# Routing and experts moved into the last image's attention, in one block

## The reference

```
x  = x + deform_conv(group_norm(x))        # 3x3 taps, each with its own (dy, dx), bilinear
t  = x as 1024 tokens
t  = t + attention(layer_norm(t))          # one causal head of 64, 1024 x 1024 scores
n  = layer_norm(t)
logits = n @ gate_w.T + gate_b             # 1024 tokens x 32 experts
probs  = softmax(logits, over the tokens)
topv, topi = top_k(probs, 8)               # each expert chooses 8 tokens
pooled[e] = sum_k topv[k, e] * n[topi[k, e]]
out[e] = gelu([pooled, 1] @ w1[e]) with 1 appended, @ w2[e]     # 65 -> 256 -> 64
t[topi[k, e]] += topv[k, e] * out[e]
```

## Time and profile before

| | us |
|---|---|
| median of 3 runs | 507.71 (504.94 to 508.09) |
| profiled execution, device time | 507.9 |
| its span in the profile | 506.1 |
| busy: PE, DVE, ACT, POOL | 416.1, 345.3, 289.8, 159.5 |
| last `back` (end of the last convolution) starts | 389.98 |
| logits of the last image start on ACT | 445.71 |
| first instruction of `route` | 452.15 |
| first matmul of `mlp` | 473.64 |
| first matmul of `combine` | 492.63 |
| last add | 499.81 |

### The profile page before, as it was taken

How to read it: one execution, slowest core, us unless ns; L and a number is a source line. 1 busy time by engine, 2 the same in 40 slices (tenths; PEclk the granted TensorE clock), 3 DMA queues, 4 the chain that set the end, 5 groups by cost and what they waited for, 6 DMA issues and landing times. The chain is left out here.

```text
span 506.1 us, 14009 instructions
## 1 busy us (share of the span) xinstructions
PE 416.1 (82%) x5845; PEld 307.5 (61%) x5845; DVE 345.3 (68%) x478; ACT 289.8 (57%) x531; POOL 159.5 (32%) x119
## 2 busy tenths in 40 slices
PE   1606985899999999999999999999999788227574
PEld 0204572576777677767767776767867556226274
DVE  3234668777898889889889989888896653213034
ACT  2323264778787687778677776877676456022100
POOL 2006007106534535472354446040640430310000
PEclk9756597999999999999999999999999969755589
DMA  9598969788787778588867789868730000039208
GB/s 221 97 208 189 222 144 231 179 205 177 188 205 177 177 183 186 123 207 195 186 160 174 175 176 207 198 158 198 181 71 12 2 2 12 1 70 229 84 3 166
DMA packets 33698, 75.61 MB, mean 149 GB/s; under 512 B 22365, under 2 KB 25373, under 8 KB 27293
## 3 DMA queue, kind: packets, MB, share of 16 engines
q1 hardware_dynamic: 28750, 72.68, 62.7%
q10 hardware_dynamic: 4880, 1.98, 1.7%
HBM read 64.74 MB, written 7.01 MB: 142 GB/s over the span
## 5 line engine op out<-in xcount | busy, mean ns | idle before, releaser
L1073 DVE TENSOR_TENSOR wring<-stage 96x640 f32<-96x640 f32 x192 | 173.0, 943 | 32.5 <-ACT stage L869 28.5
L1248 PE MATMUL psum<-wring,zring 96*64 96x160 f32 (+4 forms) x1728 | 124.8, 293 | 6.4 <-DVE wring L1073 6.4
L1248 PEld LDWEIGHTS psum<-wring,zring 96*64 96x64 f32 x1728 | 104.6, 141 | 20.9 <-issue 15.9
L1035 DVE TENSOR_REDUCE negmax<-psum 128x1 f32<-128x128 f32 (+3 forms) x64 | 48.3, 754 | 34.5 <-PE psum L1097 34.4
L1215 PE MATMUL psum<-kern,img 64*32 64x192 f32 x1536 | 58.5, 343 | 9.0 <-ACT zring L876 8.4
L876 ACT ACTIVATE zring<-psum 96x768 f32<-96x768 f32 x64 | 51.4, 803 | 23.0 <-PE psum L1215 21.4
L902 ACT ACTIVATE pT<-psum 128x512 f32<-128x512 f32 (+2 forms) x96 | 46.0, 483 | 28.4 <-PE psum L1105 28.1
L961 ACT ACTIVATE prob<-psum,negmax 128x128 f32<-128x128 f32 (+3 forms) x64 | 47.0, 734 | 22.9 <-DVE negmax L1035 18.4
L1093 PE MATMUL psum<-kT,qT 64*128 64x128 f32 (+4 forms) x400 | 51.7, 361 | 4.6 <-DVE kT L1030 1.5
L1105 PE MATMUL psum<-const,prob 128*128 128x128 f32 x288 | 50.5, 287 | 3.2 <-ACT pT L902 3.0
L866 ACT ACTIVATE stage<-stage,const 96x384 f32<-96x384 f32 x64 | 38.9, 608 | 20.5 <-DMA stage<-near 20.3
(11 more groups left out here) (120 smaller groups left out, 525.9 us busy)
## 6 DMA issues: line engine op xcount, KB each, us to landing
stage<-near SPq DMA_DIRECT2D x192, 288.0 KB, 5.5
w<-in_w SPq DMA_DIRECT2D x1, 2080.0 KB
tok<-in_x SPq DMA_DIRECT2D x8, 256.0 KB, 5.2
images<-img SPq DMA_DIRECT2D x8, 256.0 KB, 3.8
w<-in_w SPq DMA_DIRECT2D x1, 2048.0 KB
img<-img SPq DMA_DIRECT2D x7, 256.0 KB, 3.0
near<-tents SPq DMA_DIRECT2D x32, 45.0 KB
shifts<-offT SPq DMA_DIRECT2D x8, 128.0 KB, 6.4
```

Of the source, the lines that this page charges most:

```text
L1035: dve.tensor_reduce(negmax[:, t:t + 1], score_rows(t, a), AX.XY, ALU.max, negate=True).then_inc(s["mx"], 1)
L1073: dve.tensor_tensor(rows[:, ky, :, place], stage[0:KX, q % STG, ky, 1:, :], stage[0:KX, q % STG, ky, 0, :].unsqueeze(1).to_broadcast([KX, ...
L1248: ins = pe.matmul(psum[C * e:C * e + C, 2 + half, (lo % 16) * W:(lo % 16 + n) * W], zring[0:KX, q % ZRING, i % 2 * 2 + e, ky * C:(ky + 1) ...
```

## The change

There is one block. `route`, `mlp` and `combine` become the classes `Pooled` and `Experts`, whose steps are put into the last image's tables or behind the branch.

- Images are grouped 0 to 3, 4 and 5, 6 and 7 (`GROUPS`). Groups 0 and 1 (called `many`) go through choice, gather, layer 1, Gelu and the transposes inside the last image's table; their layer 2, the move, the combination and the stores come behind the branch.
- Group 2 (images 6 and 7, called `single`) does everything behind the branch. The last image's logits go from PSUM straight into rows 32 to 63 of `logits[2]`, without a DMA; the router of the last image is two matmuls of 512 columns instead of eight of 128.
- The weights are loaded by SP as soon as the last image's convolution is over, into the memory of `stage` and `wring` that it leaves. POOL zeroes `zring` and a part of `stage` there. The biases of layer 1 come as a table `b1` of 1 MB and are added by DVE; in exchange layer 1 has 64 rows and uses both halves of the array. A gather writes 16 columns (half the experts) to each half of PSUM.
- The order of the steps of all images is new in all five tables. Steady images keep the same order on POOL; on PE, ACT and DVE some neighbours change places. For image 0, ACT has `rows` 0 behind the two `tent` steps, and `rows` 1, `rows` 2 and `raw` of image 1 behind `columns` 0, which were ahead of it. For the last image, ACT has `query` ahead of image 6's `out`, and so has PE `score` 0.

```diff
@@ keep_logits @@
             sync.wait_ge(s["lg_sb"], ONE + a + 1)
+            if alone(a):
+                sync.sem_inc(s["lg_ok"], 64)
+                return
@@ act_attention @@
+                if alone(a):
+                    act.activation(by_token(logits[2][E:2 * E, :]), by_half(psum[0:E, 4:6, :]), ACT.Identity,
+                                   bias=kbias[0:E, 3:4]).then_inc(s["lg_sb"], 1)
+                    return
@@ the sync stream @@
+                    if at in table(SP_AT, b)["weights"]:
+                        sync.wait_ge(f["mm"], 2 * NG4)
+                        sync.wait_ge(f["w_ok"], K * NG4)
+                        load_weights(sync)
...
                 unless_near(sync, sync_again)
+                sync_store(sync)
+                store_last(sync, 0)
@@ new in run_all @@
+        def pe_end(pe):
+            many.layer2(pe, 0)
+            many.move(pe, 1)
+            for n in range(3):
+                pe_weigh(pe, n)
+            pooled[2].turn(pe, 0, 0)
+            pe_weigh(pe, 3)
+            pooled[2].gather(pe, 1)
+            for n in range(4, 6):
+                pe_weigh(pe, n)
+            pe.wait_ge(pooled[2].s_pT, 1)
+            single.layer1(pe)
+            for n in range(6, len(strips)):
+                pe_weigh(pe, n)
+            pe.wait_ge(s_x, len(strips))
+            for n in range(4):
+                single.turn(pe, n)
+            single.layer2(pe, 0)
+            single.move(pe, 1)
...
+            for h in range(2):
+                for t in range(NT // 2 * h, NT // 2 * h + NT // 2):
+                    ins = pe.matmul(psum[:, 2 + h, t % 4 * EXP[2]:(t % 4 + 1) * EXP[2]], pm[2][0:E * (last - first), t * P:(t + 1) * P],
+                                    eo[2][0:E * (last - first), :], start=True, stop=True)
+                ins.then_inc(s_y2, 1)
+        def act_end(act):
+            act.activation(spare[:, 1:2], ident[:, 0:1], ACT.Exp)
+            choices[2].exponentials(act)
+            act.wait_ge(s_zero, 2)
+            many.keep(act, 1, copy)
+            act.activation(spare[:, 2:3], ident[:, 0:1], ACT.Gelu)
+            pooled[2].keep_turned(act, 0, 0)
+            pooled[2].keep(act, 1)
+            for n in range(4):
+                single.gelu(act, n)
+            for n in (2, 3):
+                single.keep_turned(act, n, copy)
+            store_last(act, 1)
+        def dve_end(dve):
+            dve_choose(dve, 2, 0)
+            dve.wait_ge(s["pt"], ONE + B * NCK)
+            many.keep_out(dve, 0)
+            for step in range(1, 5):
+                dve_choose(dve, 2, step)
+            for n in range(len(strips)):
+                dve_add(dve, n)
+            for n in range(4):
+                single.add_bias(dve, n)
+            for n in range(2):
+                single.keep_turned(dve, n, dve.tensor_copy)
+            single.keep_out(dve, 0)
+            single.keep(dve, 1, dve.tensor_copy)
...
```

More of the change, by code:

```diff
@@ L75 @@
-    dict(
[L76 to L89, removed]
@@ L90 @@
-    dict(
[L91 to L104, removed]
+        turn=[-16447],
@@ L105 @@
 ACT_AT = (
     dict(
[L107 to L119, removed]
@@ L148 @@
-    dict(
[L149 to L161, removed]
+        raw=[-12735],
@@ new lines @@
+        leave=[-5039],
+        tent=[-3791, -3551],
+        columns=[-2431, -191, 753, 1185, 1234, 1505, 1729, 1811],
+        rows=[-3535, -1007, -687, 929, 1233, 1521, 1809, 1812],
+        half=[1810, 2001],
+        norm=[2465],
+        query=[2577],
+        exp=[2625, 2705, 2769, 2802, 3025, 3169, 3457, 3553],
+        prob=[2657, 2801, 2977, 3105, 3170, 3409, 3458, 3473, 3537, 3569, 3681, 3745],
+        out=[3793],
+        norm2=[4145],
+        logits=[4177],
+        choose=[],
+        pooled=[],
@@ new lines @@
+        many=[]),
+    dict(
+        raw=[-400],
+        leave=[176],
+        tent=[416, 512],
+        columns=[880, 960, 1248, 1344, 1488, 1616, 1680, 1776],
+        rows=[944, 1152, 1232, 1456, 1600, 1664, 1744, 1792],
+        half=[1936, 2288],
+        norm=[2640],
+        query=[2688],
+        exp=[2768, 2816, 2928, 3152, 3216, 3440, 3520, 3648],
+        prob=[2880, 3104, 3136, 3360, 3424, 3456, 3504, 3552, 3616, 3664, 3712, 3744],
+        out=[3792],
+        norm2=[4128],
+        logits=[4208],
+        choose=[],
+        pooled=[],
+        many=[]),
@@ new lines @@
+    dict(
+        raw=[-431],
+        leave=[209],
+        tent=[417, 497],
+        columns=[881, 930, 1234, 1361, 1425, 1553, 1650, 1729],
+        rows=[929, 1153, 1233, 1601, 1649, 1713, 1809, 2001],
+        half=[1905, 2353],
+        norm=[2673],
+        query=[2801],
+        exp=[2804, 2851, 2947, 3169, 3505, 3793, 3922, 3969],
+        prob=[2852, 2946, 3394, 3745, 3746, 3889, 3921, 3923, 3953, 4241, 4242, 4577],
+        out=[4626],
+        norm2=[6241],
+        logits=[7329],
+        choose=[],
+        pooled=[],
+        many=[]),
@@ L285, in constants @@
+    dict(
+        second=[1],
+        tents=[1106],
+        load=[1121, 1122, 1137, 1233, 2241, 2242, 2243, 2257],
+        logits=[10081],
+        weights=[4497]))
 def constants():
```

980 lines of the change are left out of this document (579 added, 401 removed).

## The result

The changed kernel takes 504.22 us in the median of 20 runs (501.16 to 508.83), the kernel before 511.21 us beside it. The ratio is 0.9905 (95% interval 0.9877 to 0.9933); a second set of six runs gave 0.9897 (0.9851 to 0.9943). So it is faster, by 1%, where 2.3% was forecast (496 us against a profiled execution of 507.9). The profiled execution took 502.84 us, span 501.0. The kernel before itself measured 3.5 us more here than the 507.7 that the forecast started from.

What follows compares the result with a forecast made beforehand. PE was taken to bound the middle, with a serial 59.9 us after image 7's logits as target. Logits at 446.2 + 1.1 + 1.4 = 448.7, plus tail 45.6, gave span 494.3; with 1.8 around it 496 us, range 488 to 504.

Steps and rivals of the forecast that it cites:

- The middle: Steady stretch bound by PE: same instructions in nearly the same order, so 0 us, bounds -3 and +4.
- The start: Images 0 and 1: image 1's statistics come later behind reordered ACT copies; net loss 1.1 us, bounds -1 and +3.
- The attention: Last image's attention: earlier `query` saves 2.4 us, inserted steps add 2.8; sum +0.4, bounds -2 and +6.
- The norm chain: Last image's norm up to its logits: inserted steps and wider logits push the end; +1.4 with the attention, bounds 0 and +9.
- The tail: Everything behind image 7's logits: branch, experts, combination and stores take 45.6 us, bounds 39 and 50.
- The Exp table: ACT behind the branch: a 1.28 us table load on the path; with the skill's 1.38 us drain, 497.4 us.
- 3 (a full branch): Branch ahead of the tail: waited out in full on ACT and PE, 5 us instead of 3; 498 us, chance 0.08.
- 1 (PE at full clock): Branch and tail: PE stays at 1.00, saving 2.0 us in layer 2 and 3.6 in the move; 490 us, chance 0.13.
- 2 (the inserted steps delay the attention by 6 us): Last image's attention: inserted steps delay it at half clock, +6 us; 502 us, chance 0.11.
- 4 (PE waits for DVE's products, 517): Middle: the new order makes PE wait up to 0.7 us at 32 pieces, 21 us; 517 us, chance 0.07.
- 5: Whole kernel: the change does little, half of rivals 4 and 2 together; 505 us, chance 0.08.
- The signs: Wrong if PE idles over 10 us between 100 and 380, `out.7` passes 440, or an engine stands over 5 us behind the branch.

Runs made afterwards that it cites:

- a0: The changed kernel run again unchanged; ratio 0.9897 to the kernel before, median 502.2 us.
- t1: The changed kernel with the tail's code inside the taken branch on every engine, and a second copy in the other arm; ratio 0.9668, 492.0 us.
- t4: The kernel of t1 with one added wait holding TensorE idle for 3.84 us ahead of layer 2; ratio 0.9864, 501.0 us.
- m1: The changed kernel with the gathering and expert steps of images 0 to 5 moved behind the last image's attention; ratio 1.0388, 526.6 us.
- h10: The changed kernel with the kernel before's order up to the end of the last convolution; ratio 0.9773, 497.6 us.
- h10b: The kernel of h10 run again; ratio 0.9777, 495.5 us.
- c1b: The kernel of c1 run again; ratio 0.9595, 487.8 us.
- c3: The changed kernel with the old order everywhere, last image included, and the tail inside the taken branch; ratio 0.9666, 490.7 us.
- x01: The kernel before with only the changed kernel's order tables, none of its new steps; ratio 1.0076, 513.2 us.
- t3: The changed kernel with the tail inside the taken branch on ScalarE alone; ratio 0.9966, 506.5 us.
- t1b: The kernel of t1 run again; ratio 0.9753, 496.2 us.
- t2: The changed kernel with the tail inside the taken branch on TensorE alone; ratio 0.9682, 492.3 us.
- s1: The changed kernel with image 0's first two column copies on ScalarE put back behind image 1's raw copy; ratio 0.9812, 499.2 us.
- c2: The kernel of t1 with the one start-order entry of s1 undone; ratio 0.9663, 491.3 us.
- c1: The changed kernel with h10's old order in front and t1's tail inside the taken branch; ratio 0.9657, 492.1 us.

## Why the prediction was wrong

The step that failed is the middle, put at 0. It covered image 7's convolution too, and there the new order costs 3.2 us in the changed kernel's trace. The whole miss in the trace, span 501.0 where the sum had 494.3, is made up of: start +0.6 (1.7 for a forecast 1.1), steady images -0.4, image 7's convolution +3.2, attention and norm chain +1.4 (2.8 for 1.4), tail +2.0 (47.6 for 45.6).

- **The middle (0).** I let PE's waits stay as they were, since the order hardly changes. One new wait of PE for DVE's products, 1.56 us, and in four of the nine traces the half clock behind it, make the last convolution 1.8 to 3.2 us longer than in before. Over seven traces of the new tables (changed, a0, t1 to t4, m1) the last back is at 393.6 to 396.0, with the old front (before, h10, h10b, c1b, c3) at 388.2 to 390.0; 391 was forecast.
- **The start (+1.1, bounds -1 and +3).** Right in direction and within its bounds against the trace of before: DVE's L514 moves from 38.62 to 42.26 (forecast 41.5), and the first back from 76.6 to 78.3. But with the same order in front the other traces have it at 73.4 to 75.0, so the start may cost 3 to 5 us; the wait of `mix` for ACT's copies is 16.1 us against 9.7 in h10 and 8.2 in before.
- **Start and middle in time.** Together they are +6.4 us (h10 and h10b against the changed kernel), or +3.9 by x01, for a forecast +1.1. With the old front the kernel measures 497.6 and 495.5, beside the forecast's 496. That is in part luck: h10's attention and norm chain are 2.6 us longer than before's where I had 1.4, and its last back is at 390.0 where I had 391.
- **The attention (+0.4, bounds -2 and +6).** The size is within its bounds: 43.4 to 44.6 us in the changed kernel, a0, t1 to t3 and both h10, and 46.2 in t4, with 42.9 before, so +0.5 to +3.3 (in the changed kernel +1.7). The reason is not borne out: I priced the inserted steps, and m1 is no faster without those on PE and ACT.
- **The norm chain (+1.4 with the attention).** From the last back to the logits it is 59.0 us in the changed kernel and in a0, 57.7 in t1, 60.0 in t4 and 56.2 before: the two steps together are +1.5 to +3.8, in the changed kernel +2.8. The first layer 1 started at 442.97, not before 438, and took 3.67 us at half clock where I had 1.8.
- **The tail (45.6, bounds 39 and 50).** The sum was right, its parts less so, and they cancelled: 47.6 and 44.2 in two traces of the changed kernel, 45.6 and 45.7 in h10 and h10b. Inside it, the branch was put at 3.0 on either engine: in the traces that jump it is 2.3 to 3.1 on ACT, and on PE 3.3 to 4.1 plus 1.6 to 2.0 inside layer 2. Layer 2 at 4.0 was right (1.50 and 2.51). The move ended 14.7 us behind the logits (forecast 13.5), and three weighs took 5.49 us at half clock where I had 2.7 at full, so they ended at 21.7 (forecast 18.0); what follows took 25.9 us where I had 27.6.
- **The Exp table.** The load takes 1.28 us in the rows. By the Trainium skill, "ScalarE: Activation LUTs", section "What ACT_TABLE_LOAD costs", 1.38 us of drain come with it. The rows of t1 do not have them: the Activate behind the load starts 0.02 us after it (452.61 after 451.31 + 1.28), and the one before ends 0.01 us ahead of it (450.19 + 1.11). The load is hidden on ScalarE anyway, as t3 shows.
- **The rivals.** 3 (a full branch) had the right place and about its price on PE, 5.4 us in two pieces for 5; what it lacked is the clock, for by t1 and t1b the 5.4 us of waiting cost 10 to 12, and t4 shows that idle time alone does so. The Trainium skill, "Runtime: NRT & Kernel Launch", section "Instruction fetch mechanics", says that a taken branch beyond the fetched window waits for a fetch of instructions; t1's trace agrees so far as the gaps of 2.38, 3.80 and 1.59 us are gone when the tail follows the branch in the code. 1 (PE at full clock) is what t1's trace shows, at 492.0 in the median, near its 490; t2, at 492.3, had half clock for some 10 us of its tail. 2 (the inserted steps delay the attention by 6 us) is out by m1. 4 (PE waits for DVE's products, 517) had the right wait, but it comes once and not at 32 pieces: three to five times too dear. 5, at 505 and 0.08, came nearest the median, for half the reason; by its own terms, half of 21 and half of 6, it should have said 509.5.
- **The signs.** None of the three signs of being wrong was met in the changed kernel's trace: PE's idle time between 100 and 380 is 8.5 us (limit 10), `out.7` came at 439.0 (limit 440; a0 has 440.1), and no gap behind the branch is over 5 us. They were too wide to catch this miss.
- **The range** (488 to 504) missed 504.22 by 0.2 us, and the second set's 502.2 lies in it. Its upper end lies just above rival 2's 502, which is reached by the order in front instead. Nothing was kept for the 2 to 3 us by which the runs of one kernel lie either side of their median, nor for a first median of the kernel before, of three runs, that was 3.5 us low.

Still open: what of s1's 4.7 us is the entry's; why the first back falls anywhere from 73.4 to 76.6 us with the same order in front; whether DVE's slow products beside POOL's norm are the cause of PE's gap in image 7, which moving POOL's step would test; and why the clock dips during the move in t2, c2 and c1b but not in t1 and c3.

## What to carry to other kernels

A branch or a wait of some 4 us on TensorE ahead of a serial tail was paid twice here: as time, and by the half clock of what follows. Put the tail's code on the path that is taken, copied into both arms, and ask of every gap on TensorE what runs right behind it. Steps put into such gaps may cost nothing, so measure the stretch without them before pricing them. An order written out anew can have its price at both ends of the pipeline even when the steady images are free: test it on the old kernel alone. And repeat a set before believing 1%: t1 gave 0.9668 and 0.9753, c1 0.9657 and 0.9595.

## What the runs showed of the hardware

TensorE alone pays for the jump in time: 3.80 and 1.59 us of "issue" in place of none, while ScalarE's 2.38 us are hidden. The second gap stands in the middle of straight code (after 46 or 47 of the 128 records in the changed kernel, a0, h10 and t3) and also goes with the jump. The granted clock falls to 0.50 behind an idle time of 3.84 us without any jump (t4). In t1 it stays at 1.00 across gaps of 1.16 and 1.56 us; in t2, with gaps of 1.10 and 1.56 us and the same instructions, it is 0.50 from 456.8 to 463.6. Two products on VectorE took 2.92 us beside two norm steps on GpSimd (1.43 and 1.50 us), and 1.73 us where those were over (1.04 us each).
